# A fused vision and text kernel on Trainium2: the LoRA product of a tile as one float32r matmul over stacked high, low and high parts

## The chip, the cores and the metric

The kernel runs on one core of one Trainium2 chip. The metric is the device time of one execution in microseconds (us), median of the executions shown. Engines are called by the profile's names: PE is TensorE's matmuls and PEld its weight loads, DVE is VectorE, ACT is ScalarE, POOL is GpSimd, SP is SyncE, which issues all of the DMA transfers. Each engine works through its own list of instructions in order; semaphores tie the lists together.

## The reference

64 images are turned into nine window tokens and a class token each (a patch convolution and two small attentions), 77 text tokens are put behind them, and the 64 x 87 tokens of 256 channels run through one attention of 16 heads with residual and one feed-forward layer with residual. What the change touches is the LoRA part of that layer, with 8 experts of rank 4 and the best two of each token:

```python
logits = x @ gate_w.T
weights, idx = jax.lax.top_k(jax.nn.softmax(logits, axis=-1), 2)
base = x @ W_lin.T + b_lin
t = jnp.einsum('nd,nkdr->nkr', x, left[idx])
out_k = jnp.einsum('nkr,nkro->nko', t, right[idx])
lora = jnp.sum(weights[..., None] * out_k, axis=1)
return (base + lora).reshape(bsz, seq, -1)      # and h = h + this
```

## The kernel before

**Two halves.** The first, `patch_tokens`, makes the window and class tokens in 5 steps and writes them to DRAM. The second, `attention_ffn`, takes the tokens in 16 groups of 4 images: 348 tokens, as 3 tiles of 116. The two halves overlap from some 215 to 270 us; from there the program is the groups'.

**The order of the work** is written out by hand. For each engine there is a table of steps (`GROUP_PE`, `GROUP_DVE`, ...) with a name, a number k and a time; `play` sorts all steps of all groups by `GROUP_START` + 276 g + time, and that order is the engine's list. So an engine works on three or more groups in turn: beside the gate and the LoRA product of one group stand the scores of the next and the projections of the one behind. A step that waits holds up all that follows in its engine's list.

**The products.** Most matmuls are split: a high part (float32r) and a low part (the rest, float32r too) of both factors, and three products hi x hi, hi x lo, lo x hi, summed in PSUM (`mm_split`, L1358, with all its matmuls on L1355). Of a group, only the attention and the LoRA product (L1474) are plain fp32, where the profile counts two records for one matmul.

**A group's end**, step by step:

- `ffn` (PE L1355, ACT L1243): one product of 116x296 a tile gives the linear part, the 32 values x @ left of all experts and the 8 logits, into `f`.
- `logits`, `rank`, `weigh` (DVE L1312 to L1335): maximum, pairwise comparisons (`g_eq` L1318, `g_gt` L1319), ranks, weights `g_w` (L1330), and `tw` (L1332): the 32 values times the weight of their expert, 96 values for the three tiles side by side.
- `base` (POOL L1150) adds the linear part to the residual.
- `twT` (PE L1466, ACT L1255): one transpose of 116x96 for all three tiles, and its copy to SBUF. Its last row is ones and takes the bias.
- `lora.0`, `lora.1` (PE L1474): for each tile one product with K = 97. `right` has for each tile its own 97 x 256 block, in which only the 32 rows of that tile and the bias row are not zero. `lora.0` does tiles 0 and 1, `lora.1` tile 2, some 14 us later. All of it goes through one PSUM bank, C (`p_c`), which `proj`, `yT`, `ffn` and the gate share; `BANKS` and `take` make the waits.
- `out` (DVE L1344) adds the product to the residual, `store` (SP L1073) writes it.

Around it stand, on DVE, `rotate` (L1279, L1282, the rotary embedding of another group's tile), `max` (L1291), `norm` (L1298, L1299), `h2` (L1304) and `stats_c` (L1309, L1310); on PE, `mT` (L1405), `scores` (L1411, L1415), `pv` (L1427), `oN` (L1435), `qkT` (L1381) and `peak` (L1397), which waits for `place`, 8 transfers by SP; on ACT the copies `oT` (L1219) and `sq` (L1186); on POOL `add` (L1115).

## Time and profile before

| | us |
|---|---|
| median of the executions | 739.92 |
| all three | 743.48, 738.27, 739.92 |
| span of the profiled execution | 734.0 |
| what the median has beyond that span | 5.9 |
| chip, cores | one Trainium2, 1 core |

The profiled execution is listed by its span alone, from the first to the last instruction; its own device time lies around that and is not given apart, so the table sets the span against the median. The page gives for each engine its busy time as a share of the span, then the chain of work that ended last, followed back through what released each piece. The timeline gives start, duration, engine, line, tiles and shapes of single instructions or of short runs (x2, x4), and in brackets the engine's idle time before and what ended it. A matmul's duration overlaps with the next one's start, so what a matmul costs its engine is read from one start to the next.

### The profile page before, as it was taken

How to read it: one execution, taken by the hardware profiler on the slowest of the kernel's cores; microseconds unless marked ns; L12 is line 12 of the kernel's file. 1: busy time of each engine (PE TensorE's matmuls, PEld its weight loads, DVE VectorE, ACT ScalarE, POOL GpSimd, SP SyncE). 2: the span in 40 equal slices, each digit the busy share in tenths (PEclk: the TensorE clock that was granted, in tenths of full speed). 3: DMA queues.
4: the chain of work that ended last, by engine and by line, in shares of the span. 5: the costliest groups of instructions: out<-in, count | busy, mean ns of one | idle time of the engine just before them, and what ended most of it. 6: DMA issues, size and time to landing. Idle time of an engine off the chain costs nothing.

```text
span 734.0 us, 24407 instructions
## 1 busy us (share of the span) xinstructions
PE 673.9 (92%) x9431; PEld 564.8 (77%) x9431; DVE 531.2 (72%) x1192; ACT 432.0 (59%) x1115; POOL 491.0 (67%) x564
## 2 busy tenths in 40 slices
PE   5998998999985799999999999999999999999873
PEld 3987887888853577888888888888888888887652
DVE  2468687887978646788878878878878887866642
ACT  4553452635442346677777676677776777776541
POOL 3667563764648428787877877876976977975442
PEclk9999999999996969999999999999999999999996
DMA  8963472231011223223232332332332332122001
GB/s 222 237 163 116 129 224 47 54 83 44 22 24 40 59 54 79 63 70 82 67 78 73 75 83 73 79 82 72 78 83 68 79 86 67 42 54 62 26 25 34
DMA packets 69528, 58.73 MB, mean 80 GB/s; under 512 B 30607, under 2 KB 68646, under 8 KB 69286
## 3 DMA queue, kind: packets, MB, share of 16 engines
q1 hardware_dynamic: 69414, 57.18, 30.9%
q8 instruction: 76, 1.25, 0.7%
q14 instruction: 38, 0.31, 0.1%
HBM read 33.69 MB, written 11.40 MB: 61 GB/s over the span
## 4 chain that ended last, share of the span: by engine, by line
PE 71%; DVE 12%; issue 4%; ACT 4%; SPq 3%; POOL 3%; DMA 2%; POOLq 0%; DVEq 0%; ACTq 0%
PE p_a L1355 13%; PE p_c L1355 10%; PE p_conv L758 8%; PE p_kv L758 7%; PE p_o L1427 6%; PE p_s L1415 5%; PE p_mm L758 4%; PE p_s L1397 4%; PE p_n L1435 3%; PE p_c L1474 3%; PE p_a L1381 3%; PE p_s L1411 2%; DVE t L1282 2%; DMA kr<-qkT 2%; DVE kv L656 1%
## 5 line engine op out<-in xcount | busy, mean ns | idle before, releaser
L1291 DVE TENSOR_REDUCE mx<-p_s 87x16 bf16<-87x1392 f32 x64 | 102.5, 1602 | 44.6 <-PE p_s L1397 44.4
L1214 ACT ACTIVATE prT<-p_s 87x1392 f32<-87x1392 f32 x64 | 85.2, 1331 | 29.3 <-PE p_s L1415 27.8
L1121 POOL TENSOR_TENSOR t<-t,ss_rs 116x512 f32<-116x512 f32 x48 | 50.9, 1060 | 58.9 <-ACT ss_rs L1190 57.8
L426 POOL TENSOR_TENSOR xs_lo<-xcols,xs_hi 120x585 fp32r<-120x585 f32 (+1 forms) x45 | 60.4, 1348 | 43.7 <-ACT xs_hi L483 43.7
L1415 PE MATMUL p_s<-qr,kr 32*87 32x87 f32 x2048 | 68.8, 257 | 0.0
L1115 POOL TENSOR_TENSOR t<-t 116x512 f32<-116x512 f32 x48 | 62.4, 1299 | 5.6 <-DVE t L1282 5.6
L1135 POOL TENSOR_TENSOR yT_lo<-y_raw,yT_hi 128x232 fp32r<-128x232 f32 x48 | 32.5, 678 | 47.1 <-issue 31.4
L1124 POOL TENSOR_TENSOR t<-t,tabs 116x512 f32<-116x512 f32 x48 | 61.2, 1276 | 2.7
L1415 PEld LDWEIGHTS p_s<-qr,kr 32*87 32x87 f32 x2048 | 60.3, 154 | 0.0
L1411 PE MATMUL p_s<-mxT,pick_row 32*87 32x87 bf16 x1024 | 55.7, 208 | 1.9 <-ACT mxT L1208 1.9
L1427 PE MATMUL p_o<-prT,vp 87*32 87x87 f32 x2048 | 55.1, 248 | 0.1
L1427 PEld LDWEIGHTS p_o<-prT,vp 87*32 87x32 f32 x2048 | 43.9, 142 | 9.8 <-issue 3.2
L1130 POOL TENSOR_TENSOR onT_lo<-on_raw,onT_hi 128x174 fp32r<-128x174 f32 x64 | 37.0, 586 | 20.2 <-ACT onT_hi L1226 11.9
L1186 ACT ACTIVATE sq<-p_a 116x512 f32<-116x512 f32 x48 | 28.8, 600 | 36.5 <-PE p_a L1355 36.4
L440 POOL TENSOR_TENSOR red<-red,pe 117x256 f32<-117x256 f32 (+1 forms) x35 | 27.5, 785 | 31.9 <-ACT pe L491 30.9
L515 ACT COPY kv<-p_kv 117x512 f32<-117x512 f32 (+1 forms) x45 | 26.6, 590 | 30.9 <-PE p_kv L758 30.9
L1279 DVE TENSOR_TENSOR t<-p_a,tabs 116x512 f32<-116x512 f32 x48 | 32.9, 685 | 15.4 <-ACT sq L1186 15.4
L1435 PE MATMUL p_n<-ident,oT 128*87 128x128 f32 x256 | 40.2, 280 | 1.2 <-ACT onT_hi L1226 1.2
L1411 PEld LDWEIGHTS p_s<-mxT,pick_row 32*87 32x87 bf16 x1024 | 32.5, 117 | 11.5 <-issue 5.1
L1204 ACT ACTIVATE vt<-p_a,a_rs 116x256 f32<-116x256 f32 x48 | 22.6, 474 | 28.4 <-PE p_a L1355 28.4
L758 PE MATMUL p_conv<-w_conv_hi,xs_hi 120*117 120x256 f32 (+1 forms) x225 | 38.1, 299 | 0.0
L1397 PE MATMUL p_s<-kr,qr 32*87 32x88 f32 x1024 | 33.3, 256 | 4.3 <-ACT prT L1214 2.1
(287 smaller groups left out, 2077.8 us busy)
## 6 DMA issues: line engine op xcount, KB each, us to landing
xcols<-in_x_cols SPq DMA_DIRECT2D x12, 822.7 KB, 8.1
h<-h_tokens SPq DMA_DIRECT2D x16, 348.0 KB
out<-out_sb SPq DMA_DIRECT2D x48, 116.0 KB
h_tokens<-in_txt SPq DMA_DIRECT2D x4, 1232.0 KB, 8.7
x<-in_txt_cols SPq DMA_DIRECT2D x32, 154.0 KB, 4.1
qr<-qkT SPq DMA_DIRECT2D x64, 58.0 KB, 2.0
kr<-qkT SPq DMA_DIRECT2D x64, 58.0 KB, 2.0
vp<-vt SPq DMA_DIRECT2D x32, 87.0 KB
```

The source lines that it names most:

```text
L426: nc.gpsimd.tensor_tensor(xs.lo[:, n % XS_SLOTS, :, 0:M].bitcast(F32R), raw, xs.hi[:, n % XS_SLOTS, :, 0:M], ALU.subtract).then_inc(S['xs_ ...
L758: mm_ = nc.tensor.matmul(out, a, b, start=(c == 0), stop=(c == len(lhs) - 1))
L1115: link(nc.gpsimd.tensor_tensor(t1[:, b], t1[:, b], t2[:, b], ALU.add))
L1124: nc.gpsimd.tensor_tensor(by_head(t1[:, b]), by_head(t1[:, b]), table(2, k), ALU.add).then_inc(S['rope_ok'], 1)
L1214: nc.scalar.activation(prT[:, k % 2], p_s[0:SEQ, :, 0:QUADS * SEQ], ACT.Exp, scale=HD ** -0.5).then_inc(S['s_exp'], 1)
L1291: nc.vector.reduce_max(mx[:, k % 2, :, 0:QUADS], p_s[0:SEQ, :, 0:QUADS * SP].rearrange("p j (a k) -> p j a k", k=SP)[:, :, :, 0:SEQ], AX_X ...
L1355: mm_ = nc.tensor.matmul(out, a, b, start=(c == 0), stop=(c == len(lhs) - 1))
L1397: mm_ = nc.tensor.matmul(p_s[0:SEQ, j, a * SP:(a + 1) * SP], rows(qr, j, a, SEQ).bitcast(F32R), rows(kr, j, a, SP).bitcast(F32R), start=Tr ...
L1411: nc.tensor.matmul(p_s[0:SEQ, j, a * SEQ:(a + 1) * SEQ], pick_row[ROW * j:ROW * (j + 1), a], mxT[ROW * j:ROW * (j + 1), k % 2], start=True ...
L1415: mm_ = nc.tensor.matmul(p_s[0:SEQ, j, a * SEQ:(a + 1) * SEQ], rows(kr, j, a, SEQ), rows(qr, j, a, SEQ), start=False, stop=True, skip_grou ...
L1427: mm_ = nc.tensor.matmul(p_o[ROW * j:ROW * (j + 1), a * SEQ:(a + 1) * SEQ], vp[:, half, k, :, 4 * a + j], prT[:, k % 2, j, a * SEQ:(a + 1) ...
L1435: mm_ = nc.tensor.transpose(p_n[0:SEQ, c * P:(c + 1) * P], oT[:, k % 2, c], ident[:])
```

## The change

The LoRA product becomes float32r, high and low parts in one matmul. `tw` holds three copies of a tile's 32 values side by side (96 columns a tile), and each tile is transposed by itself, so that a tile's 96 rows stand ready in one column range of `twT`. ScalarE casts all 96 rows to float32r (the high part). VectorE's new step `tw_lo` writes the low part over rows 32 to 63. Two rows of ones take the bias. The other factor, `right_3`, holds high, high and low part of `right` and of the bias; it is made once. One float32r matmul with K = 98 is then high x high + low x high + high x low. `right` has one block in place of three.

```diff
--- before.py
+++ after.py
...
@@ -96,7 +97,7 @@
         self.w_v = Split(sb("w_v_hi", [P, CC, C]), sb("w_v", [P, CC, C]))
         self.w_p = sb("w_p", [P, CC, C])
         self.w_f = sb("w_f", [P, CC, FFN_N])
-        self.right = sb("right", [TILES * LR + 1, TILES, C])
+        self.right, self.right_hi, self.right_3 = (sb(n, [LORA_K, C]) for n in ("right", "right_hi", "right_3"))
         self.b_proj = sb("b_proj", [P, C])
         self.mean_row = sb("mean_row", [P, P])
         self.ones = sb("ones", [P, P])
...
@@ -129,17 +130,15 @@
         sp.dma_start(self.rope_in[:], io['rope']).then_inc(self.S['rope_in'], 16)
         sp.dma_start(self.rope_g[:], io['rope_g'].unsqueeze(0).broadcast_to([TP, 8, HD])).then_inc(self.S['rope_in'], 16)
 
-    LOADS = 3 + 1 + TILES + 1
+    LOADS = 3 + 1 + 3 + 1
 
     def load_weights(self, nc, sp, io):
         sources = (io['w_qkv'][:, 0:2 * C], io['w_qkv'][:, 2 * C:3 * C], io['w_ffn'], io['w_proj'])
         for w, source in zip(self.uncentred + [self.w_p[:]], sources):
             sp.dma_start(w, source.rearrange("(k p) n -> p k n", p=P)).then_inc(self.w_in, 16)
-        sp.wait_ge(self.S['zeroed'], 1)
-        for t in range(TILES):
-            sp.dma_start(self.right[LR * t:LR * (t + 1), t], io['right']).then_inc(self.w_in, 16)
-        sp.dma_start(self.right[TILES * LR:TILES * LR + 1], io['rows'][TOKEN_ROWS + 1:TOKEN_ROWS + 2].unsqueeze(1).broadcast_to(
-            [1, TILES, C])).then_inc(self.w_in, 16)
+        for n in range(3):
+            sp.dma_start(self.right[LR * n:LR * (n + 1)], io['right']).then_inc(self.w_in, 16)
+        sp.dma_start(self.right[3 * LR:LORA_K], io['rows'][TOKEN_ROWS + 1].unsqueeze(0).broadcast_to([2, C])).then_inc(self.w_in, 16)
 
     def fill_early(self, nc, pool, link):
 
@@ -149,7 +148,6 @@
         link(nc.gpsimd.memset(self.ident[:], 0.0))
         nc.gpsimd.affine_select(out=self.ident[:], in_=self.ident[:], compare_op=ALU.not_equal, fill=1.0, base=0,
                                 pattern=[[-1, P]], channel_multiplier=1).then_inc(self.S['filled'], 1)
-        nc.gpsimd.memset(self.right[:], 0.0).then_inc(self.S['zeroed'], 1)
 
     def fill_late(self, nc, pool, link):
 
@@ -913,7 +911,7 @@
 GROUP_DVE = table("""stats.0.-202 stats.1.-176 stats.2.-169 eps.0.-130 rotate.0.-17 ss.0.43 rotate.1.58 ss.1.114 rotate.2.173
                 ss.2.201 max.0.292 max.1.361 max.2.427 max.3.499 norm.0.522 norm.1.561 norm.2.603 norm.3.688
                 h2.0.733 h2.1.749 stats_c.0.791 stats_c.1.805 h2.2.861 stats_c.2.866 logits.0.950 rank.0.996
-                weigh.0.1038 out.0.1104 out.1.1109 out.2.1248""")
+                weigh.0.1038 tw_lo.0.1092 out.0.1104 out.1.1109 out.2.1248""")
 GROUP_PE = table("""qk.0.-48 qk.1.19 v.0.84 qkT.0.131 qk.2.148 qkT.1.194 v.1.211 qkT.2.277 peak.0.281 mT.0.315 scores.0.325
                 peak.1.353 mT.1.378 scores.1.388 pv.0.412 peak.2.419 mT.2.444 scores.2.453 oN.0.475 peak.3.482
                 pv.1.497 mT.3.520 pv.2.522 scores.3.529 oN.1.548 oB.0.569 oN.2.587 oB.1.611 pv.3.622 oB.2.651
...
@@ -981,8 +979,9 @@
         g_max, g_sum, g_rs = sb("g_max", [TP, TILES]), sb("g_sum", [TP, TILES]), sb("g_rs", [TP, TILES])
         g_e, g_rank, g_w = (sb(n, [TP, TILES, EXPERTS]) for n in ("g_e", "g_rank", "g_w"))
         g_gt, g_eq = (sb(n, [TP, TILES, EXPERTS, EXPERTS]) for n in ("g_gt", "g_eq"))
-        tw = sb("tw", [TP, TILES, LR])
+        tw = sb("tw", [TP, TILES, 3 * LR])
         out_sb = sb("out_sb", [TP, TILES, C])
+        twT = sb("twT", [LORA_K, TILES, TP])
 
         p_a = ps("p_a", [P, 512])
         p_s = ps("p_s", [P, 4, 512])
...
@@ -1089,7 +1088,6 @@
                 pool.wait_ge(W['stat'], CONVS)
                 pool.wait_ge(W['red'], (CELLS - 1) * STEPS)
                 ready(nc.gpsimd.memset(vp[:, :, :, HD:], 1.0))
-                ready(nc.gpsimd.memset(twT[TILES * LR:TILES * LR + 1], 1.0))
 
             def step(name, g, k):
                 half, b = g % 2, (3 * g + k) % 2
@@ -1143,6 +1141,15 @@
                         for n, (w, raw) in enumerate(((wp, w_p), (wf, w_f))):
                             pool.wait_ge(S['w2_high'], n + 1)
                             nc.gpsimd.tensor_tensor(w.lo[:].bitcast(F32R), raw[:], w.hi[:], ALU.subtract).then_inc(S['w2_low'], 1)
+                        pool.wait_ge(S['w2_low'], 2)
+                        pool.wait_ge(W['cls_ok'], STEPS)
+                        ready(nc.gpsimd.memset(twT[3 * LR:LORA_K], 1.0))
+                        pool.wait_ge(S['w2_high'], 3)
+                        lows = slice(2 * LR, LORA_K)
+                        ready(nc.gpsimd.tensor_tensor(right_3[lows].bitcast(F32R), right[lows], right_hi[lows], ALU.subtract))
+                        bias = slice(3 * LR, 3 * LR + 1)
+                        nc.gpsimd.tensor_copy(right_3[bias].bitcast(F32R), right_hi[bias]).then_inc(S['w2_low'], 1)
+                        pool.wait_ge(S['w2_low'], 3)
                     wait(pool, S['h2_ok'], 3 * (g - 1) + k + 1)
                     nc.gpsimd.tensor_tensor(hb[:, k], h[:, g % H_SLOTS, k], consts.b_proj[0:TP], ALU.add).then_inc(S['hb_ok'], 1)
                 if name == 'base':
@@ -1168,6 +1175,8 @@
                         act.wait_ge(consts.S['w_sub'], 3 * CC)
                         nc.scalar.copy(wp.hi[:].bitcast(F32R), w_p[:]).then_inc(S['w2_high'], 1)
                         nc.scalar.copy(wf.hi[:].bitcast(F32R), w_f[:]).then_inc(S['w2_high'], 1)
+                        nc.scalar.copy(right_3[0:2 * LR].bitcast(F32R), right[0:2 * LR])
+                        nc.scalar.copy(right_hi[:].bitcast(F32R), right[:]).then_inc(S['w2_high'], 1)
                     wait(act, S['a_var'], 3 * g + 3)
                     wait(act, S['v_out'], TILES * (g - 1))
                     link(nc.scalar.activation(a_ln[:, half], a_mv[:, half, :, 1], ACT.Ln, bias=eps5[0:TP, 0:1]))
@@ -1252,7 +1261,8 @@
                 if name == 'twT':
                     wait(act, S['twT_ok'], g + 1)
                     wait(act, S['lora'], 2 * g)
-                    nc.scalar.copy(twT[0:TILES * LR], product('gate', g, k)[0:TILES * LR, 0:TP]).then_inc(S['twT_out'], 1)
+                    nc.scalar.copy(twT[0:3 * LR].bitcast(F32R), product('gate', g, k)[0:3 * LR, 0:GT].rearrange("p (t n) -> p t n", t=TILES)
+                                   ).then_inc(S['twT_out'], 1)
 
             return step
 
@@ -1329,10 +1339,18 @@
                     link(nc.vector.reciprocal(g_rs[:], g_sum[:]))
                     link(nc.vector.tensor_tensor(g_w[:], g_w[:], g_rs[:].unsqueeze(2).broadcast_to([TP, TILES, EXPERTS]),
                                                  ALU.mult))
-                    nc.vector.tensor_tensor(
-                        tw[:].rearrange("p t (e r) -> p t e r", r=RANK),
-                        f[:, half, :, C:C + LR].rearrange("p t (e r) -> p t e r", r=RANK),
-                        g_w[:].unsqueeze(3).broadcast_to([TP, TILES, EXPERTS, RANK]), ALU.mult).then_inc(S['tw_ok'], 1)
+                    shape = [TP, 3, EXPERTS, RANK]
+                    for tile in range(TILES):
+                        last = nc.vector.tensor_tensor(
+                            tw[:, tile].rearrange("p (n e r) -> p n e r", n=3, r=RANK),
+                            f[:, half, tile, C:C + LR].rearrange("p (e r) -> p e r", r=RANK).unsqueeze(1).broadcast_to(shape),
+                            g_w[:, tile].unsqueeze(1).unsqueeze(3).broadcast_to(shape), ALU.mult)
+                    last.then_inc(S['tw_ok'], 1)
+                if name == 'tw_lo':
+                    dve.wait_ge(S['twT_out'], g + 1)
+                    lows = slice(LR, 2 * LR)
+                    nc.vector.tensor_tensor(twT[lows].bitcast(F32R), product('gate', g, k)[lows, 0:GT].rearrange("p (t n) -> p t n", t=TILES),
+                                            twT[lows], ALU.subtract).then_inc(S['tw_low'], 1)
                 if name == 'out':
                     dve.wait_ge(S['lora'], 2 * g + k // 2 + 1)
                     dve.wait_ge(S['fb_ok'], n3)
@@ -1461,17 +1479,20 @@
                     mm_split(product('tile', g, k)[0:TP, 0:FFN_N], yT.chunks(lambda x_, c: x_[:, b, c]), wf.chunks(lambda x_, c: x_[:, c])
                              ).then_inc(S['ffn'], 1)
                 if name == 'twT':
-                    use(bank('gate', g, k), S['twT_out'], g + 1)
+                    use(bank('gate', g, k), S['tw_low'], g + 1)
                     pe.wait_ge(S['tw_ok'], g + 1)
-                    nc.tensor.transpose(product('gate', g, k)[0:TILES * LR, 0:TP], tw[:].rearrange("p t n -> p (t n)"),
-                                        ident[0:TP, 0:TP]).then_inc(S['twT_ok'], 1)
+                    for tile in range(TILES):
+                        mm_ = nc.tensor.transpose(product('gate', g, k)[0:3 * LR, TP * tile:TP * (tile + 1)],
+                                                  tw[:, tile], ident[0:TP, 0:TP])
+                    mm_.then_inc(S['twT_ok'], 1)
                 if name == 'lora':
                     use(bank('lora', g, k), S['out_ok'], 3 * g + LORA_TILES[k][-1] + 1)
                     if g == 0 and k == 0:
-                        pe.wait_ge(S['set_0'], TW_SET)
-                    pe.wait_ge(S['twT_out'], g + 1)
+                        pe.wait_ge(S['w2_low'], 3)
+                    pe.wait_ge(S['tw_low'], g + 1)
                     for n, tile in enumerate(LORA_TILES[k]):
-                        mm_ = nc.tensor.matmul(product('lora', g, k)[0:TP, n * C:(n + 1) * C], twT[:], right[:, tile], start=True, stop=True)
+                        mm_ = nc.tensor.matmul(product('lora', g, k)[0:TP, n * C:(n + 1) * C], twT[:, tile].bitcast(F32R),
+                                               right_3[:].bitcast(F32R), start=True, stop=True)
                     mm_.then_inc(S['lora'], 1)
 
             return step
```

The order of the instructions around group 7's end, first TensorE at the transpose `twT` (the rows after the transpose are `mT`, `pv` and the first of `scores`), before:

```order
L1466 MATMUL p_c<-ident,tw 96x116 [waits b_tw_ok,b_yT_out]
L1405 MATMUL p_s<-ident_b,mx 128x87 [waits b_s_max]
L1427 MATMUL p_o<-prT,vp 32x87 [waits l_v_in0,l_v_in1,b_s_exp,b_o_out]
L1427 MATMUL p_o<-prT,vp 32x87 x15
L1411 MATMUL p_s<-mxT,pick_row 87x87 [waits b_mT_out]
```

and with the change:

```order
L1485 MATMUL p_c<-ident,tw 96x116 [waits b_tw_ok,b_yT_out]
L1485 MATMUL p_c<-ident,tw 96x116 x2
L1423 MATMUL p_s<-ident_b,mx 128x87 [waits b_s_max]
L1445 MATMUL p_o<-prT,vp 32x87 [waits l_v_in0,l_v_in1,b_s_exp,b_o_out]
L1445 MATMUL p_o<-prT,vp 32x87 x15
L1429 MATMUL p_s<-mxT,pick_row 87x87 [waits b_mT_out]
```

Two transposes more, and nothing else moved. Next TensorE at `lora.0` (ahead of it the end of `scores`, behind it `oN` and `qkT`), before:

```order
L1411 MATMUL p_s<-mxT,pick_row 87x87 x4
L1415 MATMUL p_s<-qr,kr 87x87 x4
L1474 MATMUL p_c<-right,twT 116x256 [waits b_twT_out]
L1474 MATMUL p_c<-right,twT 116x256
L1435 MATMUL p_n<-ident,oT 87x128 [waits b_o_out,b_o_norm]
L1435 MATMUL p_n<-ident,oT 87x128 x3
L1381 MATMUL p_a<-ident,t 128x116 [waits b_rope_ok,b_rot_ok]
```

and with the change:

```order
L1429 MATMUL p_s<-mxT,pick_row 87x87 x4
L1433 MATMUL p_s<-qr,kr 87x87 x4
L1494 MATMUL p_c<-right,twT 116x256 [waits b_tw_low]
L1494 MATMUL p_c<-right,twT 116x256
L1453 MATMUL p_n<-ident,oT 87x128 [waits b_o_out,b_o_norm]
L1453 MATMUL p_n<-ident,oT 87x128 x3
L1399 MATMUL p_a<-ident,t 128x116 [waits b_rope_ok,b_rot_ok]
```

The pair of products stands where it stood, and waits for `tw_low`, VectorE's new step, in place of ScalarE's copy. Last VectorE between `norm` and `out.0` (`c_st` is `stats_c`, `t` is `rotate`), before:

```order
L1298 RECIPROCAL rd<-p_n 87x16 [waits b_oB,b_oN]
L1299 TENSOR_TENSOR on<-p_n,rd 87x256 [waits k_dve_1]
L1309 BN_STATS c_st<-h 116x6 [waits b_h2_ok]
L1310 BN_AGGR c_mv<-c_st 116x2 [waits k_dve_1]
L1279 TENSOR_TENSOR t<-p_a,tabs 116x512 [waits b_qkT_ok,b_sq_ok]
L1282 TENSOR_TENSOR t<-p_a,tabs 116x32x8 x2
L1344 TENSOR_TENSOR out_sb<-p_c,h 116x256 [waits stored0,b_fb_ok,b_lora]
```

and with the change:

```order
L1308 RECIPROCAL rd<-p_n 87x16 [waits b_oB,b_oN]
L1309 TENSOR_TENSOR on<-p_n,rd 87x256 [waits k_dve_1]
L1319 BN_STATS c_st<-h 116x6 [waits b_h2_ok]
L1320 BN_AGGR c_mv<-c_st 116x2 [waits k_dve_1]
L1289 TENSOR_TENSOR t<-p_a,tabs 116x512 [waits b_qkT_ok,b_sq_ok]
L1292 TENSOR_TENSOR t<-p_a,tabs 116x32x8 x2
L1352 TENSOR_TENSOR twT<-p_c,twT 32x348 [waits b_twT_out]
L1362 TENSOR_TENSOR out_sb<-p_c,h 116x256 [waits stored0,b_fb_ok,b_lora]
```

`tw_lo` (L1352) has come in behind `rotate` and ahead of `out.0`.

## Rows read from the trace of the kernel before

**Rows 1.** The page, parts 1 and 4: busy us (share of the span) xinstructions; chain shares.

```profile
PE 673.9 (92%) x9431; PEld 564.8 (77%) x9431; DVE 531.2 (72%) x1192; ACT 432.0 (59%) x1115; POOL 491.0 (67%) x564
...
PE 71%; DVE 12%; issue 4%; ACT 4%; SPq 3%; POOL 3%; DMA 2%; POOLq 0%; DVEq 0%; ACTq 0%
```

**Rows 2.** One stretch: length, busy PE, PEld, DVE, ACT, POOL, clock, DMA share, GB/s.

```profile
330.00:640.00 310.00, 306.83 (x5564) 261.87 (x5560) 252.35 (x571) 224.26 (x581) 244.89 (x297) 1.00 0.29 75
```

**Rows 3.** Waits, 330 to 640 us: total us, times, longest.

```profile
DVE h L1304 <- PE p_c L1355: 11.6, 11, 1.1
DVE out_sb L1344 <- PE p_c L1474: 8.1, 11, 0.8
...
PEld p_s L1397 <- issue: 1.6, 4, 0.6
...
PE p_s L1397 <- DMA kr<-qkT: 0.7, 2, 0.4
```

**Rows 4.** Timeline, TensorE's matmuls: start us, us, engine, line, xcount [idle before <-releaser].

```profile
520.49 0.49 PE L1355 MATMUL p_c<-w_p_hi,onT_hi 128*116 128x256 f32 x2 [0.19 <-DVE h L1304]
520.82 0.40 PE L1355 MATMUL p_c<-w_p_lo,onT_hi 128*116 128x256 f32 x2
521.05 0.41 PE L1355 MATMUL p_c<-w_p_hi,onT_lo 128*116 128x256 f32 x2
...
526.24 0.26 PE L1466 MATMUL p_c<-ident,tw 116*96 116x116 f32 x1
526.34 0.20 PE L1405 MATMUL p_s<-ident_b,mx 87*128 87x87 bf16 x1
...
528.30 1.12 PE L1474 MATMUL p_c<-right,twT 97*116 97x256 f32 x4
529.26 0.60 PE L1435 MATMUL p_n<-ident,oT 128*87 128x128 f32 x4
...
542.64 0.60 PE L1474 MATMUL p_c<-right,twT 97*116 97x256 f32 x2
543.08 0.56 PE L1381 MATMUL p_a<-ident,t 116*128 116x116 f32 x4
```

**Rows 5.** Timeline, VectorE, 519 to 531 us and at 670 us.

```profile
523.92 0.26 DVE L1332 TENSOR_TENSOR tw<-f,g_w 116x96 f32<-116x96 f32 x1
524.09 1.60 DVE L1291 TENSOR_REDUCE mx<-p_s 87x16 bf16<-87x1392 f32 x1
...
527.34 0.69 DVE L1279 TENSOR_TENSOR t<-p_a,tabs 116x512 f32<-116x512 f32 x1
527.95 0.75 DVE L1282 TENSOR_TENSOR t<-p_a,tabs 116x256 f32<-116x256 f32 x2
529.46 0.76 DVE L1344 TENSOR_TENSOR out_sb<-p_c,h 116x256 f32<-116x256 f32 x2 [0.76 <-PE p_c L1474]
...
669.88 0.76 DVE L1344 TENSOR_TENSOR out_sb<-p_c,h 116x256 f32<-116x256 f32 x2 [1.62 <-PE p_c L1474]
```

**Rows 6.** Lines L1330, L1319 (ns min/median/max); timeline of GpSimd.

```profile
L1330 DVE TENSOR_TENSOR g_w<-g_w,g_rs x16: 182/946/990, 325.4 to 723.8; 116x24 f32<-116x24 f32 x16
...
L1319 DVE TENSOR_TENSOR g_gt<-f x16: 350/651/655, 316.3 to 721.1; 116x192 f32<-116x192 f32 x16
...
521.33 0.72 POOL L1150 TENSOR_TENSOR h<-h,f 116x256 f32<-116x256 f32 x1
...
522.52 1.32 POOL L1115 TENSOR_TENSOR t<-t 116x512 f32<-116x512 f32 x1
523.92 0.86 POOL L1150 TENSOR_TENSOR h<-h,f 116x256 f32<-116x256 f32 x1
```

**Rows 7.** Timeline, ScalarE, the copies twT and oT.

```profile
527.20 0.26 ACT L1255 COPY twT<-p_c 96x116 f32<-96x116 f32 x1
527.39 0.45 ACT L1219 COPY oT<-p_o 128x348 f32<-128x348 f32 x1
```

**Rows 8.** Timeline, TensorE in group 14.

```profile
711.74 1.09 PE L1474 MATMUL p_c<-right,twT 97*116 97x256 f32 x4 [0.43 <-ACT twT L1255]
```

11 lines of the change are left out of this document (6 added, 5 removed).

## The prediction

> **What bounds the kernel now.** I read the page first. TensorE is busy 92% of the span and carries 71% of the chain that ended last [rows 1]. Nearly all of the change's work lies in the group stage, so the stretch of 330 to 640 us comes next: there TensorE is busy 306.8 of 310.0 us at full clock, VectorE 252.4, ScalarE 224.3, GpSimd 244.9 [rows 2]. TensorE has no idle time to speak of; the others have some. The waits of that stretch (11 group periods of some 28 us) say where [rows 3]: VectorE waits for TensorE at the projection's `h2` (1.06 us a group) and at the LoRA product (0.74 us a group), and TensorE waits for the `place` transfers before `peak` in a few groups, 0.7 us seen on the matmuls and 1.6 us on the weight loads.
>
> So a shorter LoRA product is worth its time only if its inputs are there. That is asked of the timeline of one group. TensorE starts `twT` at 526.24, reaches `lora.0` at 528.30 and leaves it at 529.26 [rows 4]. VectorE, which has no part between `tw` and the LoRA product before the change, is at that moment in `rotate`: its three instructions run from 527.34 to 528.70, and the first of them follows on other work without a gap [rows 5]. The place repeats from group to group: VectorE's wait for the product is 0.74 us in the mean of 11 groups and at most 0.8 [rows 3]. The new step `tw_lo` stands in VectorE's list between that `rotate` and `out.0`, and `lora.0` waits for it.
>
> **TensorE.** Before, a product of 116x256 is two records; a pair of products holds the engine from 528.30 to 529.26, 0.96 us, and the single one of `lora.1` from 542.64 to 543.08, 0.44 us [rows 4]. A float32r product of the same 256 columns is there in the projection: two take 0.23 us from 520.82 to 521.05, and 0.33 us where they come out of a wait (520.49 to 520.82) [rows 4]. So `lora.1` gives back 0.44 - 0.12 = 0.32 us, `lora.0` 0.96 - 0.23 = 0.73 us if it finds its input ready, 0.63 us if it waits. Two more transposes a group cost 0.10 us each (526.24 to 526.34) [rows 4]. Without any wait that is 0.32 + 0.73 - 0.20 = 0.85 us a group and 13.6 us in 16.
>
> **ScalarE.** The copy `twT` grows from 116 to 348 columns: 0.26 to 0.45 us, the latter being the time of the `oT` copy of 348 columns [rows 7]. It ends near 527.9 instead of 527.46. VectorE is in `rotate` until later, so this costs nothing in a steady group. In group 14, whose steps follow one another, it costs its 0.19.
>
> **VectorE: `tw`.** One instruction of 96 elements becomes three. They follow one another at 0.17 us (523.92 to 524.09) [rows 5]: +0.34 us. The bare price is not all. `g_w` of 24 elements takes 0.18 us at its least and 0.95 at the median of 16, and in the steady group `tw`, which waits for it, starts at 523.92, just behind the end of GpSimd's `add` at 522.52 + 1.32 = 523.84 [rows 5, 6]. `g_gt` takes 0.35 us at its least and 0.65 at the median, again in groups with GpSimd at work, and it is the second of two instructions issued together [rows 6]. Right at `tw` GpSimd starts `base` (523.92) and needs 0.86 us where the instruction before it of the same line took 0.72 [rows 6]: it was held 0.14 us by `tw`. I read it so: an instruction of VectorE that reads two operands from SBUF, and one of GpSimd, keep each other out, and one that has been waiting goes ahead of VectorE's next. Then the first `tw` goes, `base` follows it, and the second `tw` waits for most of 0.72 us. Bounds are 0 and 0.77 (what `g_w` loses); from the nearest case, `g_gt`, which loses 0.30 us to a GpSimd instruction of two thirds of the size, I take 0.50. Together `tw` makes VectorE 0.84 us later in each of the groups 0 to 11.
>
> This is also what the Trainium skill says, page SBUF — State Buffer, section Who interferes with whom: an instruction of VectorE with two inputs in SBUF contends with one of GpSimd that reads SBUF, and the second to issue is blocked until the first has finished; `tw_lo` and `out` read one operand from PSUM and are free of it. The rows on `g_w` and `g_gt` agree. Without this rule the sum would be the second case below, with it the first.
>
> **VectorE: `tw_lo`.** It reads 348 elements from PSUM. By `out_sb` (two of 256 in 0.76, so 0.42 for one) and `rotate`'s first (512 in 0.69) [rows 5] it takes 0.42 + 92 x 0.27/256 = 0.52 us.
>
> **The wait.** In the row's group, before: `rotate` starts 527.34 and its successor could start 1.29 us later. Now: 527.34 - 0.03 (it waited for nothing longer) + 0.84 = 528.15, `tw_lo` from 529.44 to 529.96, TensorE 0.06 us behind, as after a late `h2`, so `lora.0` at 530.02 and the next step at 530.35 instead of 529.26: **+1.09 us**. TensorE alone would have been at `lora.0` at 528.50; the other 1.5 us it stands still. Queued behind are `oN`, `qkT`, `peak` and the projection. `peak` has waits of its own for the transfers of `place`, whose start doesn't move; of these waits, 0.7 to 2.3 us in all, I let 1.6 be swallowed. VectorE is later by about 1.1 us at `max.0` too, but it waits 1 us or more for TensorE twice before the group ends [rows 3], so nothing is carried over. A steady group is thus longer by 1.09 - 0.32 = 0.77 us: 12 x 0.77 - 1.6 = **+7.6 us**.
>
> **The tail.** Groups 12 and 13 have no `rotate` ahead; VectorE waits 1.62 us for the product there [rows 5]. Between 0 and -0.85 us each; I take -0.35, as half lies beside a wait for a transfer. In group 14 TensorE waits for the copy `twT` [rows 8], so its chain runs through every added piece: +0.34 and 0.50 (`tw`), 0.20, 0.19, 0.58 (`tw_lo` and its signal), less 0.63: **+1.2 us**. In group 15 the same additions, near 1.8, meet the three products at the end of the program, which give back some 1.1 and more at a lower clock: 0, within 0.9. Sum of the tail: +0.5.
>
> **Setup.** ScalarE makes two more copies and GpSimd three small instructions, once, and GpSimd is busy 67% of the span [rows 1]; the memset of `right` goes and as many transfers stay. At most 3 x 0.72 = 2.2 us by `base`'s row [rows 6], at least 0; I take 0, for GpSimd's own waits cover it, and keep the rest for the range.
>
> **Sum: +8.1 us.** The profiled execution spans 734.0 us, 5.9 less than the median of the runs; I carry the difference over: 739.9 + 8.1 = **748.0 us**. Case ends: with 0 for the held `tw` the steady group is 0.50 us less, with 0.77 it is 0.27 more: 742.0 and 751.2; rounding the transfers' share and the setup in, 741 to 753.
>
> **Rivals.**
> 1. **The three `tw` are not held** by `base`. Then a steady group changes by +0.27 us, group 14 by +0.7: 12 x 0.27 - 1.6 + 0 = +1.6, **741.6 us**. For it: `tw` itself shows 0.26 us and went ahead of `base`. Against: `g_gt`, in the same position, is held in most groups. Chance 0.27.
> 2. **The saving arrives**, the other side. The place is `rotate`'s end: if VectorE finished `tw_lo` by 528.44, 1.5 us before my figure, TensorE would not wait, and all of 0.85 us a group would come: 726.3 us. Half of that way is plausible: a GpSimd a little later would neither hold `g_w` (0.77 us) nor `tw` (0.50), leaving `lora.0` at 528.75 and a group shorter by 0.18 + 0.32 = 0.50 us: -6.0 with -0.7 for groups 12 and 13, **733.2 us**. It decides where VectorE is ahead by over 0.77 us of my figure. For it: TensorE is the busiest engine and loses 17 us of work. Against: offsets that repeat in 12 groups, with `g_w` held every time. Chance 0.15.
> 3. **A second hold**: GpSimd's next instruction, moved by the first, meets the third `tw` or the pushed `max` and `norm`, 0.5 us more a group: **754 us**. Against: GpSimd is idle a fifth of the stretch [rows 2], so another instruction need not stand ready. Chance 0.13.
>
> My forecast has 0.45. That the products aren't cheaper isn't a case: the same form runs in the projection [rows 4].
>
> **Numbers.** Under 1% (7.4 us) a measurement of this kernel can't be told from no change. The forecast lies at its edge: of its 0.45, 0.26 is slower and 0.19 the same. Rival 1: the same, 0.01 to slower, 0.02 to faster. Rival 2: 0.10 faster, 0.05 the same. Rival 3: slower, 0.13. Faster 0.12, same 0.48, slower 0.40. The forecast's own range is 741 to 753; to hold 8 in 10, with half of the second rival and of the third, it is 733 to 755.
>
> **What would show it.** Right: in most groups TensorE idles over 1 us before the LoRA pair, released by `tw_lo`; records of that line fall to a half; the second `tw` takes near 0.7 us and the others 0.26; `base` still 0.86; VectorE's wait before `out_sb` all but gone; the group period up from 310.0/11 = 28.2 us by 0.8. Wrong: a wait under 0.5 us before the pair (rival 2), `tw` at 0.26 three times and the wait near 1.0 (rival 1), or TensorE waiting for `max` as well (rival 3). What would upset it most is `tw_lo` being done before `rotate`'s end, or a chain of waits that runs through another step of the group than this one.

## The result, and the profile after

The changed kernel takes **771.96 us** (median of 4 runs, 769.02 to 773.53) against 740.54 us (738.27 to 743.48); the ratio is 1.045, 95% interval 1.0403 to 1.0497. Ratios are of fast executions alone, so they differ a little from those of the medians (here 1.042). The kernel is slower, as the likeliest case had it, but by 31.4 us and not by 8.1, and outside the range. The profiled execution spans 769.8 us, 35.8 more than before.

The page, parts 1, 2 and 4 (the clock is in tenths of full speed, one digit for a fortieth of the span), to be read against [rows 1]:

```profile
span 769.8 us, 24428 instructions
PE 684.3 (89%) x9415; PEld 575.4 (75%) x9415; DVE 557.0 (72%) x1240; ACT 433.8 (56%) x1117; POOL 492.3 (64%) x565
...
PEclk9999999999988689999899899999899999999875
...
PE 62%; DVE 23%; issue 6%; ACT 4%; POOL 2%; DMA 2%; SPq 1%; DVEq 0%; POOLq 0%; ACTq 0%
```

VectorE's share of the chain that ended last has risen from 12% to 23%. And the clock row shows an 8 at several places in the group stage, where before it was 9 throughout. The stretches (length, busy PE, PEld, DVE, ACT, POOL, clock, DMA share, GB/s), the first against [rows 2], then three groups from one transpose `twT` to the next, and the second of them in part:

```profile
330.00:640.00 310.00, 290.17 (x5118) 247.42 (x5117) 249.88 (x555) 205.75 (x533) 225.42 (x272) 0.95 0.28 71
330.30:359.80 29.50, 27.52 (x510) 23.47 (x509) 24.74 (x56) 20.53 (x53) 22.39 (x28) 1.00 0.29 74
359.80:392.50 32.70, 30.41 (x509) 25.99 (x508) 25.03 (x56) 20.51 (x53) 22.32 (x28) 0.90 0.25 65
392.50:421.90 29.40, 27.50 (x509) 23.48 (x508) 24.63 (x56) 20.52 (x53) 22.38 (x28) 1.00 0.30 76
...
364.00:371.00 7.00, 6.53 (x39) 5.72 (x40) 4.90 (x10) 1.50 (x6) 2.30 (x4) 0.51 0.28 77
```

So there are two kinds of group. Five of eleven take 29.4 to 29.5 us at a clock of 1.00, which is 1.2 more than 28.2; six take 30.9 to 32.7 us at 0.89 to 0.94. In the longest, TensorE stands still from about 362.6 to 364.5 us (1.83 us, 0.35 more than in the others), and from the end of that standstill it works for some 7 us at half clock (1.2 instead of 2.4 GHz). At full clock the work of those 7 us would have taken about half of the time. The group is 3.3 us longer than its neighbours: 0.35 for the longer standstill and some 2.9 for the clock.

The waits of the stretch (total us, times, longest), against [rows 3]:

```profile
PE p_c L1494 <- DVE twT L1352: 15.1, 10, 1.8
DVE h L1314 <- PE p_c L1373: 10.6, 10, 1.1
DVE out_sb L1362 <- PE p_c L1494: 7.2, 10, 0.9
PEld p_s L1423 <- DVE mx L1301: 6.3, 17, 0.6
PE p_s L1423 <- DVE mx L1301: 2.8, 11, 0.3
```

The first row is the predicted wait: 1.5 us a group, in every group, released by `tw_lo`. The last two rows are `mT` waiting for `max`; before, there were 0.5 us of that in the stretch, on the weight loads alone. VectorE in one steady group, from the projection's `h2` to `out`, against [rows 5]:

```profile
387.79 0.42 DVE L1314 TENSOR_TENSOR h<-p_c,hb 116x256 f32<-116x256 f32 x1 [1.06 <-PE p_c L1373]
...
388.81 0.41 DVE L1338 SCALAR_TENSOR_TENSOR g_w<-g_rank,g_e 116x24 f32<-116x24 f32 x1
389.25 0.18 DVE L1339 RECIPROCAL g_rs<-g_sum 116x3 f32<-116x3 f32 x1
389.46 1.00 DVE L1340 TENSOR_TENSOR g_w<-g_w,g_rs 116x24 f32<-116x24 f32 x1
390.50 1.14 DVE L1344 TENSOR_TENSOR tw<-f,g_w 116x96 f32<-116x96 f32 x3
391.56 1.59 DVE L1301 TENSOR_REDUCE mx<-p_s 87x16 bf16<-87x1392 f32 x1
...
394.78 0.67 DVE L1289 TENSOR_TENSOR t<-p_a,tabs 116x512 f32<-116x512 f32 x1
395.37 0.75 DVE L1292 TENSOR_TENSOR t<-p_a,tabs 116x256 f32<-116x256 f32 x2
396.15 0.51 DVE L1352 TENSOR_TENSOR twT<-p_c,twT 32x348 fp32r<-32x348 f32 x1
397.31 0.76 DVE L1362 TENSOR_TENSOR out_sb<-p_c,h 116x256 f32<-116x256 f32 x2 [0.65 <-PE p_c L1494]
```

From `h2` to the start of the `rotate` it is 6.99 us, before 5.84 (521.50 to 527.34). The three `tw` take 1.14 us together (predicted 1.10), `tw_lo` 0.51 (0.52). What I had not priced is the first `g_w`, 0.41 instead of 0.18 us. TensorE's end of it, against [rows 4]:

```profile
392.52 0.46 PE L1485 MATMUL p_c<-ident,tw 116*96 116x116 f32 x3
393.22 0.21 PE L1423 MATMUL p_s<-ident_b,mx 87*128 87x87 bf16 x1 [0.23 <-DVE mx L1301]
...
396.81 0.47 PE L1494 MATMUL p_c<-right,twT 98*116 98x256 f32 x2 [1.49 <-DVE twT L1352]
397.11 0.60 PE L1453 MATMUL p_n<-ident,oT 128*87 128x128 f32 x4
```

The pair of products holds TensorE for 0.30 us instead of 0.96, but it stands behind a standstill of 1.49 us.

Where the 35.8 us lie, by the starts of `twT`: 2.0 had been lost when the first group reached it (330.30 against 328.34), 26.4 in the next eleven groups, 7.4 in the rest. The 26.4 divide into 12.9 (eleven groups of 29.45 us in the mean of the undisturbed five, less 311.06 us) and 13.5 (what the six groups at low clock are longer than 29.45).

### The profile page after: what moved, and what is told of

The parts are those of the page before. It is cut to its first block, busy times and chain, and to the rows that moved or that the text cites. A ratio compares the mean times of both kernels' runs of the same rounds, so it can differ in the third digit from the quotient of the medians.

```text
span 769.8 us, 24428 instructions
## 1 busy us (share of the span) xinstructions
PE 684.3 (89%) x9415; PEld 575.4 (75%) x9415; DVE 557.0 (72%) x1240; ACT 433.8 (56%) x1117; POOL 492.3 (64%) x565
## 3 DMA queue, kind: packets, MB, share of 16 engines
q1 hardware_dynamic: 69412, 57.18, 29.4%
## 4 chain that ended last, share of the span: by engine, by line
PE 62%; DVE 23%; issue 6%; ACT 4%; POOL 2%; DMA 2%; SPq 1%; DVEq 0%; POOLq 0%; ACTq 0%
PE p_a L1373 12%; PE p_c L1373 10%; PE p_conv L756 7%; PE p_kv L756 5%; PE p_s L1433 4%; PE p_mm L756 4%; PE p_o L1445 4%; PE p_s L1415 3%; PE p_n L1453 3%; DVE mx L1301 3%; DVE t L1292 3%; PE p_a L1399 2%; DVE tw L1344 2%; DVE g_w L1340 2%; PE p_s L1429 1%
## 5 line engine op out<-in xcount | busy, mean ns | idle before, releaser
L1433 PE MATMUL p_s<-qr,kr 32*87 32x87 f32 x2048 | 70.5, 261 | 0.0
L1133 POOL TENSOR_TENSOR yT_lo<-y_raw,yT_hi 128x232 fp32r<-128x232 f32 x48 | 32.7, 683 | 52.7 <-issue 31.1
L438 POOL TENSOR_TENSOR red<-red,pe 117x256 f32<-117x256 f32 (+1 forms) x35 | 27.5, 785 | 31.5 <-ACT pe L489 30.5
L1289 DVE TENSOR_TENSOR t<-p_a,tabs 116x512 f32<-116x512 f32 x48 | 32.7, 682 | 15.9 <-ACT sq L1195 15.7
L1453 PE MATMUL p_n<-ident,oT 128*87 128x128 f32 x256 | 42.9, 293 | 1.2 <-ACT onT_hi L1235 1.2
L1204 ACT COPY qkT<-p_a 128x464 f32<-128x464 f32 x48 | 26.1, 543 | 29.4 <-PE p_a L1399 29.3
L1373 PE MATMUL p_a<-w_qk_hi,xT_hi 128*116 128x512 f32 x96 | 38.0, 480 | 1.0 <-ACT qkT L1204 0.6
```

What stands on the lines that cost most here:

```text
L1373: mm_ = nc.tensor.matmul(out, a, b, start=(c == 0), stop=(c == len(lhs) - 1))
L1433: mm_ = nc.tensor.matmul(p_s[0:SEQ, j, a * SEQ:(a + 1) * SEQ], rows(kr, j, a, SEQ), rows(qr, j, a, SEQ), start=False, stop=True, skip_grou ...
L1453: mm_ = nc.tensor.transpose(p_n[0:SEQ, c * P:(c + 1) * P], oT[:, k % 2, c], ident[:])
```

## The experiments

Twelve kernels. **Theory W**: the late `tw_lo` makes TensorE stand still, which costs its length, and a standstill of that length also lets the clock fall, which costs about as much again. **Rival L**: the clock falls because there is less TensorE work, or for a cause outside the wait. Ratios are to the kernel before, on the same chip, with a 95% interval.

**1. `tw_lo` ahead of the `rotate`.**

```diff
-                weigh.0.1038 tw_lo.0.1092 out.0.1104
+                weigh.0.1038 tw_lo.0.1086 out.0.1104
```

> The changed kernel with one number altered: tw_lo stands in VectorE's list ahead of the rotate instead of behind it. In the changed kernel's trace a group takes 29.4 us where the granted clock is 1.00 throughout and 30.9 to 32.7 us in six of eleven groups, in which the clock falls to 0.50 right in or behind the 1.5 us that TensorE stands still before the LoRA pair. Theory W (the standstill costs its own length, and it also brings the clock down): tw_lo ends 0.5 us after the copy twT, TensorE waits under 0.2 us, no group runs at the low level, a group takes 27.6 to 28.0 us and the kernel 730 to 738 us. Rival L (the clock falls because TensorE has less work a group, or for a cause outside this wait): the wait goes, 1.2 us a group come back, but some groups still run at 0.50 and the kernel takes 750 to 758 us. Rival Q (the rotate, now 0.5 us later, delays qkT or max by as much as is won): a group stays at 28.6 us or more at full clock, 744 us or more.

749.44 us, ratio 1.0074 (1.0025 to 1.0124). One number takes the loss from 4.5% to 0.7%. Clock and waits of the stretch:

```profile
330.00:640.00 310.00, 298.07 (x5465) 252.42 (x5463) 265.76 (x595) 220.16 (x570) 239.55 (x292) 1.00 0.29 74
```
```profile
PE p_a L1399 <- DVE t L1292: 4.3, 11, 0.4
PE p_s L1423 <- DVE mx L1301: 2.8, 11, 0.3
PE p_c L1494 <- DVE twT L1352: 2.2, 10, 0.2
```

No group of the stretch is at the low level, as W says and L denies. But a group takes 28.75 us, not 27.8: rival Q. TensorE now waits 0.4 us for the `rotate`, 0.25 for `max`, 0.2 for `tw_lo`, together nearly a microsecond a group, so at this place too VectorE's added work is paid for.

**2. A first try to fill the standstill.**

```diff
+                    if k == 0:
+                        for n in range(12):
+                            nc.tensor.matmul(product('lora', g, k)[0:TP, 0:C], wp.hi[:, 0, 0:TP]..., wp.hi[:, 0]..., ...)
                     pe.wait_ge(S['tw_low'], g + 1)
```

> The changed kernel with twelve float32r products of 116x256 on constant weights ahead of lora.0, into the columns that lora.0 then overwrites; TensorE works through the 1.4 us in which it stood still, all waits and data stay. Theory W: the lateness of tw_lo is unchanged, so a group stays at 29.4 us, but the clock stays at 1.00 in 330 to 640 us; the 13.8 us of the long groups and some 4 us of the tail go, 752 to 758 us. Rival L (another cause of the low clock): groups of 31 to 33 us remain, 768 us or more. If the fillers themselves delay lora.0 (over 1.5 us long), each 0.1 us costs 1.5 us in all.

776.71 us, ratio 1.0475 (1.0398 to 1.0551). A miss of construction: `use` ahead of the fillers already waits for `tw_low`, as the bank is the gate's. The wait of 1.38 us stayed and the fillers came behind it, so a group at full clock is 30.7 us and the three at a low clock are 32.1 to 32.7. As a test of W the run says nothing. But that the clock was 1.00 in eight of eleven groups here, with the standstill in all of them, is the first sign that the standstill alone doesn't decide.

**3. One `tw` in place of three.**

```diff
-                    for tile in range(TILES):
-                        last = nc.vector.tensor_tensor(tw[:, tile]..., f[:, half, tile, C:C + LR]..., g_w[:, tile]..., ALU.mult)
+                    link(nc.vector.tensor_tensor(g_wr[:]..., g_w[:].unsqueeze(3)..., g_rs[:]..., ALU.mult))
+                    nc.vector.tensor_tensor(tw[:]..., f[:, half, :, C:C + LR].unsqueeze(2)..., g_wr[:].unsqueeze(2)..., ALU.mult)
```

> The changed kernel with the weights spread to 96 elements in the last g_w instruction, so that one tw instruction of 288 elements takes the place of three of 96. Theory H (the second tw is held by GpSimd's base for about 0.5 us): g_w and tw together take 0.6 us less, the wait before lora.0 falls from 1.5 to 0.9 us, a full-clock group from 29.4 to 28.8 us. With the clock still falling in half the groups that is 760 to 765 us; if a standstill of 0.9 us no longer brings it down, 745 to 750 us. Rival (three instructions were slow by themselves, not held): the one instruction gives 0.2 us a group or less, 768 us or more.

766.36 us, ratio 1.0343 (1.0268 to 1.0418). The 0.6 us did not come. In a steady group:

```profile
383.98 1.08 DVE L1342 TENSOR_TENSOR g_wr<-g_w,g_rs 116x96 f32<-116x96 f32 x1
385.10 0.98 DVE L1345 TENSOR_TENSOR tw<-f,g_wr 116x288 f32<-116x288 f32 x1
```

The one `tw` is issued just behind GpSimd's `base` (385.02) and held as a whole; in the tail, where no `base` runs, the same instruction takes 0.46 us. So the hold is real, but folding three into one doesn't evade it. TensorE still stands 1.47 us, and nine of eleven groups ran at 0.89 to 0.94, where the changed kernel with the same standstill had six.

**4. The wait alone, in the kernel before.**

```diff
+                if name == 'late':
+                    dve.wait_ge(S['twT_out'], g + 1)
+                    nc.vector.tensor_tensor(spare[:], product('gate', g, k)[0:LR, 0:TP]..., twT[0:LR]..., ALU.subtract)...
-                    pe.wait_ge(S['twT_out'], g + 1)
+                    pe.wait_ge(consts.S['zeroed'], g + 2)
```

> The kernel before, with its fp32 products, its one tw and its one transpose, and one thing added: an instruction of VectorE of tw_lo's size (32x348, one operand from PSUM, result unused) at tw_lo's place behind the rotate, and both LoRA products wait for it. No work of TensorE changes. Its end should come at 0.98 us behind the point at which TensorE reaches lora.0. Theory W: TensorE stands still 0.9 to 1.0 us a group, a full-clock group takes 29.0 to 29.2 us, and the clock falls in some groups as in the changed kernel: 757 to 770 us. Rival L (the low clock comes from the smaller products): the wait costs its length only, 750 to 753 us, clock 1.00 in the group stage.

752.95 us, ratio 1.0147 (1.0073 to 1.0222). TensorE waits 0.87 us in a group, a group is 29.06 us, and the clock is 1.00 in all eleven. By this run alone L was alive: a wait without lighter products, and no low clock.

**5. The work of `tw` alone, in the kernel before.**

```diff
+                    for n in range(2):
+                        nc.vector.tensor_tensor(spare[:, n]..., f[:, half, :, C:C + LR]..., g_w[:]..., ALU.mult)
```

> The kernel before with two more instructions of tw's size and inputs ahead of tw (results unused), so that VectorE has the three that the change gives it; TensorE's work, the transposes and the LoRA products stay fp32 and wait for what they waited for. It tests the step of my forecast by which lateness of VectorE is not carried over while it doesn't meet the LoRA wait. If that holds: the second instruction is held by base as in the changed kernel (three in 1.1 us), mT waits 0.1 to 0.2 us for max in a group, a group takes 28.2 to 28.4 us, 740 to 745 us. Rival (VectorE and TensorE form a loop from h2 to the rotate and mT in which any VectorE work costs its length): a group of 28.8 us or more, 750 us or more.

747.03 us, ratio 1.0116 (1.0049 to 1.0183). The least of its groups are 28.49 us, 0.3 more than 28.15, with TensorE never waiting for anything in the LoRA step. "Nothing is carried over" is off by at least 0.3 us a group, between the two expectations and nearer to the first. The mean of the eleven is 28.81 us against 28.28 before, but this trace is of the longest execution (754.35 us) and has two waits for transfers, 0.63 and 1.16 us, in it.

**6. The wait doubled.**

```diff
-                    nc.vector.tensor_tensor(spare[:]..., ALU.subtract).then_inc(consts.S['zeroed'], 1)
+                    for n in range(2):
+                        last = nc.vector.tensor_tensor(spare[:, n]..., ALU.subtract)
+                    last.then_inc(consts.S['zeroed'], 1)
```

> The fourth kernel (before, plus an unused instruction of tw_lo's size that the LoRA products wait for) with two such instructions instead of one. That one stood TensorE still for 1.0 us a group, its groups took 29.06 us at a granted clock of 1.00. Now the standstill is 1.5 us, as long as in the changed kernel, while all of TensorE's products are those of before. Theory W (the length of the standstill decides whether the clock falls): some groups of 31 to 33 us beside groups of 29.5 us, mean clock in 330 to 640 us 0.95, 766 us or more. Rival L (the clock falls only with the lighter float32r products): all groups 29.5 us at 1.00, 757 to 762 us.

767.15 us, ratio 1.0327 (1.0239 to 1.0415). The trace is of the longest of the four executions, 771.14 us; the shortest took 757.65. Three groups:

```profile
448.60:478.10 29.50, 28.00 (x511) 23.91 (x510) 23.83 (x55) 20.44 (x53) 22.37 (x28) 1.00 0.29 75
507.60:540.90 33.30, 31.29 (x510) 26.39 (x509) 24.69 (x58) 20.61 (x53) 22.31 (x28) 0.90 0.25 65
570.40:602.50 32.10, 29.85 (x510) 25.09 (x509) 24.62 (x58) 20.51 (x53) 22.30 (x28) 0.95 0.25 68
```

All of TensorE's work is the fp32 work of before, and the clock falls in three of eleven groups: L is refuted as far as lighter products go. The standstill is 1.3 us in most groups and 1.6 to 1.8 in four; the three low groups are among the four. The group behind the eleven is low too (0.94), with a standstill of only 1.31 us. In the first of the three, VectorE, TensorE, and the clock us by us:

```profile
503.86 1.33 DVE L1329 SCALAR_TENSOR_TENSOR g_w<-g_rank,g_e 116x24 f32<-116x24 f32 x1
```
```profile
511.77 1.09 PE L1482 MATMUL p_c<-right,twT 97*116 97x256 f32 x4 [1.76 <-DVE spare L1341]
```
```profile
511.00:512.00 1.00, 0.23 (x1) 0.26 (x2) 0.63 (x2) 0.41 (x1) 1.00 (x3) 1.00 0.21 60
512.00:513.00 1.00, 1.00 (x7) 0.83 (x7) 0.10 (x1) 0.00 (x0) 1.00 (x1) 1.00 0.11 35
513.00:514.00 1.00, 1.00 (x11) 0.71 (x13) 0.97 (x4) 0.06 (x1) 0.18 (x1) 0.68 0.12 38
514.00:515.00 1.00, 1.00 (x18) 0.92 (x19) 0.56 (x2) 0.89 (x3) 0.00 (x0) 0.50 0.23 65
```

A `g_w` of 24 elements took 1.33 us, beside a GpSimd `add` that began with it, where it takes 0.17 in the groups around; the standstill grew to 1.76, and only after it the clock fell. The order in time excludes that the low clock makes the wait.

**7. The standstill filled.**

```diff
+                if name == 'lora' and k == 0 and g < GROUPS - 3:
+                    for bank_ in BANKS['N']:
+                        pe.wait_ge(*freed[bank_])
+                    for n in range(11):
+                        nc.tensor.matmul(p_n[0:TP, 0:C], wp.hi[:, 0, 0:TP]..., wp.hi[:, 0]..., start=True, stop=True)
```

> The changed kernel with eleven float32r products of 116x256 on constant weights, some 1.3 us, ahead of lora.0 in TensorE's list, this time into the bank of the transposed outputs, which is free then, so that they don't wait for tw_lo (in the first try they stood behind that wait). tw_lo comes when it came. Theory W: the wait left before lora.0 is 0.2 to 0.4 us, the groups take 29.4 us throughout at a clock of 1.00, 752 to 758 us. Rival (the clock falls for another reason than the standstill): groups of 31 us and more stay, 768 us or more.

756.32 us, ratio 1.021 (1.0133 to 1.0287). The stretch, and one group:

```profile
330.00:640.00 310.00, 305.51 (x5466) 262.32 (x5463) 259.13 (x581) 215.52 (x558) 233.66 (x285) 1.00 0.29 73
416.30:445.70 29.40, 28.98 (x520) 24.86 (x519) 24.62 (x56) 20.49 (x53) 22.40 (x28) 1.00 0.29 74
```

This is the separating run. Nothing is faster: `tw_lo` is as late, a group takes 29.3 to 29.8 us. Only TensorE is busy where it stood still, with work that nobody uses, and all eleven groups keep 1.00. By the ratios the loss falls from 4.5% to 2.1%; the medians, 771.96 and 756.32, lie 15.6 us apart. Of the 18.8 us by which this trace is longer than the one before the change, 12.6 are the lateness itself, in the eleven groups, and 6.9 lie behind them, where the last three groups have no fillers and the clock falls again (the first `twT` comes 0.6 us earlier).

**8. A candidate.** As 1 and 3 together, and `weigh` behind `max.3`, so that `g_w` and `tw` don't meet GpSimd's `add` and `base`.

```diff
-                weigh.0.1038 tw_lo.0.1092 out.0.1104
+                weigh.0.1052 tw_lo.0.1086 out.0.1104
```

> A candidate: tw_lo ahead of the rotate, one tw of 288 elements with the weights spread to 96, and weigh behind max.3 instead of ahead of it, so that VectorE makes max (which reads PSUM) while GpSimd's add runs, and g_w is not held 0.8 us by it. In e1 a group takes 28.75 us with mT waiting 0.25 us for max and qkT 0.4 us for the rotate. If g_w and tw are no longer held, VectorE is 1 us a group shorter, these waits go, and a group takes 27.6 to 28.0 us: 728 to 738 us, faster than before. If they are held all the same (by base, which follows add), or twT now waits for tw, 28.3 to 28.8 us: 742 to 750 us.

743.82 us, ratio 1.0005 (0.9957 to 1.0053): as before, and not the 728 to 738 us that were hoped for. In a group:

```profile
555.25 0.36 DVE L1339 SCALAR_TENSOR_TENSOR g_w<-g_rank,g_e 116x24 f32<-116x24 f32 x1
...
555.86 0.26 DVE L1342 TENSOR_TENSOR g_wr<-g_w,g_rs 116x96 f32<-116x96 f32 x1
556.15 0.46 DVE L1345 TENSOR_TENSOR tw<-f,g_wr 116x288 f32<-116x288 f32 x1
```

1.08 and 0.98 us have become 0.26 and 0.46. A group takes 28.0 us, 0.2 less than before, but three of the last ones lose 7.4 us (27.7, 28.0 and 23.4 against 26.8, 26.1 and 18.8), with waits for `tw` of 1.1 and 1.5 us and clocks of 0.94 and 0.64 in the last two of them.

**9. The same with `weigh` at its old place in the last four groups.**

```diff
-    turns += [(GROUP_START + GROUP_PERIOD * g + time, ...)
+    turns += [(GROUP_START + GROUP_PERIOD * g + (1038 if name == 'weigh' and g >= GROUPS - 4 else time), ...)
```

> e8_reordered with weigh at its old place in the last four groups. e8's steady groups take 28.01 us against 28.2 of the kernel before, but its last groups are longer (27.7, 28.0 and 23.4 us against 26.8, 26.1 and 18.8), where TensorE waits for tw 1.1 and 1.5 us, since max now stands ahead of it and no add of GpSimd is there any more to be avoided, and where the clock is 0.94 and 0.64. Expected: the waits for tw go in these groups, 2 to 7 us less than e8: 736 to 741 us, a ratio to before of 0.990 to 0.998. If the lower clock of the end doesn't come from these waits (TensorE also waits 1.2 and 1.4 us for max there, in every kernel of the study), less than 2 us are won: 741 to 744 us.

742.24 us, ratio 1.0018 (0.9977 to 1.0058), 1.6 us below experiment 8 by the medians, which is the expectation's second case and within the noise. The waits for `tw` are gone (26.7 us for the first of these groups), but two later ones stay long (28.7 and 20.1) at clocks of 0.88 and 0.85. One steady group of this kernel, beside its neighbour, and TensorE's waits in that neighbour:

```profile
411.90:439.90 28.00, 27.43 (x509) 23.40 (x509) 23.24 (x54) 20.52 (x53) 22.24 (x28) 1.00 0.30 78
439.90:470.90 31.00, 29.13 (x510) 24.84 (x510) 23.50 (x54) 20.51 (x53) 22.25 (x28) 0.94 0.29 73
```
```profile
PE p_s L1415 <- DMA kr<-qkT: 1.3, 1, 1.3
PE p_a L1399 <- DVE t L1294: 0.4, 1, 0.4
```

A wait of 1.3 us for a `place` transfer, in a kernel whose LoRA product doesn't wait, and the clock falls within a microsecond behind it. The cause need not be `tw_lo`; a standstill of that size can do it.

**10. `qkT.2` behind `peak.0`.**

```diff
-                qk.2.148 qkT.1.194 v.1.211 qkT.2.277 peak.0.281
+                qk.2.148 qkT.1.194 v.1.211 qkT.2.282 peak.0.281
```

> e9 with qkT.2 behind peak.0 in TensorE's list. In e8 TensorE waits 0.39 us a group there for the rotate that tw_lo now stands ahead of. If that wait is on the path, a group falls from 28.0 to 27.6 or 27.7 us, 4 us less than e9: 731 to 737 us. If max.0, or the place transfers that follow qkT, then come too late, 28.0 us or more, and no gain.

749.28 us, ratio 1.0123 (1.0075 to 1.0171). The wait for the `rotate` is gone, and a group still takes 28.04 us: TensorE waits instead for the exponential (3.7 us in the stretch) and for the transfers, which start later (5.4 us in five places, the longest 1.5, with the clock at 0.94 in that group).

**11. The changed kernel with `weigh` behind `max.3` and nothing else.**

```diff
-                weigh.0.1038 tw_lo.0.1092 out.0.1104
+                weigh.0.1052 tw_lo.0.1092 out.0.1104
```

> The changed kernel with one number altered: weigh stands behind max.3 in VectorE's list; three tw instructions and tw_lo behind the rotate stay. Theory H (of the lateness of tw_lo, 0.24 us at the first g_w, 0.8 at the last, and 0.5 at tw are VectorE held by GpSimd's add and base): out of add's way these go, tw_lo ends 1.3 to 1.5 us earlier, TensorE waits at most 0.3 us for it, the clock stays at 1.00 and a group takes 27.9 to 28.2 us: 740 to 747 us with the longer tail of e8. Rival (base holds them at the new place as well): wait 0.7 to 1.0 us, 28.8 us, 748 to 755 us.

752.54 us, ratio 1.0151 (1.0084 to 1.0219); the trace is of the longest execution, 758.87 us. The time lies where the rival had it, but not for the rival's reason. The holds at the last `g_w` and at `tw` are gone:

```profile
535.04 0.42 DVE L1338 SCALAR_TENSOR_TENSOR g_w<-g_rank,g_e 116x24 f32<-116x24 f32 x1
...
535.70 0.18 DVE L1340 TENSOR_TENSOR g_w<-g_w,g_rs 116x24 f32<-116x24 f32 x1
535.92 0.60 DVE L1344 TENSOR_TENSOR tw<-f,g_w 116x96 f32<-116x96 f32 x3
```

1.00 us is 0.18 and 1.14 us is 0.60, so 1.36 us of VectorE were GpSimd's doing, 0.54 of it new with the change. Yet TensorE still waits 1.15 us. VectorE now waits 0.47 us for `max`'s own input, so that from `h2` to the `rotate` it is 6.21 us, only 0.78 less than in the changed kernel, and that is also what a group is shorter (28.6 us for 29.4). Of the eleven, the one with a wait of 1.5 us ran at low clock.

**12. The order of 9 in the kernel before**, a control.

> The kernel before with weigh behind max.3 except in the last four groups, as in e9: a control that says how much of e9's time is due to the order and not to the LoRA change. TensorE is busy 28.0 of 28.2 us there, so freeing VectorE can give at most 0.2 us a group: 738 to 742 us, ratio 0.995 to 1.002.

741.77 us, ratio 1.0031 (1.0002 to 1.006). The order gives nothing where TensorE is the bound. So 9 and 12 are level: with the float32r products in the best order I found, the LoRA change is worth nothing measurable. This run also shows the low clock without any part of the change. In one group TensorE waits for a `place` transfer, and the group takes 31.5 us where its neighbours take 28.2 and 28.5:

```profile
415.93:447.46 31.53, 29.61 (x510) 25.04 (x509) 22.52 (x52) 20.56 (x53) 22.17 (x28) 0.95 0.28 71
```
```profile
PE p_s L1398 <- DMA kr<-qkT: 1.7, 1, 1.7
```

What the kernels show together, for the eleven groups from the first `twT` on:

| kernel | usual longest standstill of a group, us | groups under 1.00 |
|---|---|---|
| before | 0.2, once 0.4 | 0 |
| 7, filled | 0.2, twice 0.3 | 0 |
| 5, `tw` alone | 0.2, once 1.16 | 0 |
| 12, order alone | 0.2, once 1.72 | 1 (that one) |
| 1, `tw_lo` first | 0.4, once 0.5 | 0 |
| 8, candidate | 0.4, once 0.7 | 0 |
| 9, tail order | 0.4, once 1.31 | 1 (that one) |
| 10, `qkT` later | 0.6, once each 1.01 and 1.23, once 1.52 | 1 (the last) |
| 4, wait alone | 0.87, once 1.24 | 0 |
| 11, `weigh` behind | 1.15, once 1.50 | 1 (that one) |
| 6, wait doubled | 1.30, four of 1.60 to 1.77 | 3 (of the four) |
| 2, fillers behind | 1.38, once 1.73 | 3 (that one and two more) |
| 3, one `tw` | 1.47 | 9 |
| changed kernel | 1.48, once 1.83 | 6 (that one and five more) |

No group whose longest standstill is under 1.3 us is at a low clock. In all 25 low groups the clock falls in a standstill of 1.31 us or more, or within 2 us of its end.

## Why the prediction was wrong

**Right**: that the saving would not arrive, and why. In every steady group TensorE stands before the LoRA pair for `tw_lo`; the wait was put at 1.5 us and is 1.48. The pair holds TensorE for 0.30 us, for 0.96 before. The second `tw` was held by `base` (three in 1.14 us, 1.10 predicted), `base` still takes 0.86, and experiment 11 shows the hold by taking `add` and `base` away. `tw_lo` takes 0.51 us against 0.52. VectorE's wait before `out_sb` did not vanish as I wrote: 0.65 us instead of 0.76, since VectorE now waits there for the pair that its own `tw_lo` has only just released. (Where the prediction says which of its cases goes with a hold and which without, it counts loosely: with a hold it is the forecast, without it rival 1.)

**The step that failed** is the price of the wait. The sum took "the other 1.5 us it stands still" at its length and left the clock at the 1.00 of [rows 2]. In the trace the clock falls in six of eleven groups in that standstill or just behind it, which is 13.5 us, and more in the tail. Experiments 6 and 7 separate it: standstills of 1.6 us and more bring low groups with all the old work in place, and the changed kernel with the standstill filled has none in these eleven and is 15.6 us faster. No rival held this case. The profiled execution is 35.8 us longer where 8.1 were forecast; 13.5 of the 27.7 us between are here. The kernel before had the low level in its rows too, at 0.83 between 210 and 300 us and at 0.82 and 0.50 in its last two groups; the prediction thought of it at the program's end alone.

**A second term was too small**: a steady group was to be 0.77 us longer, less what transfers' waits swallow, and is 1.2. From `h2` to the `rotate` VectorE is 1.15 us later, not 0.84 less 0.03. The rows name 0.23 us at the first `g_w`, 0.05 at the second, 0.04 at `tw`; `tw_lo` starts 1.37 us behind the `rotate` and not 1.29, and TensorE 0.15 us behind its end and not 0.06. The 0.23 is "a second hold", my third rival, on an instruction I hadn't looked at, and that rival's sign, TensorE waiting for `max` as well, is there with 0.25 us a group. For the hold: GpSimd stands 0.3 us later against VectorE than before, and its `onT_lo` (388.61 to 389.18) meets `g_w`. That `onT_lo` is what holds it rests on the overlap alone; in experiment 11 the first `g_w` still took 0.42, with `base` (534.68 to 535.42) then beside it.

**"Nothing is carried over"** held only nearly. Experiment 5 puts `tw`'s work into the kernel before, where no LoRA step waits for it, and finds 0.3 us a group. The prediction leaned on two waits of 1 us or more by [rows 3]; these rows have 1.05 us at `h2` and 0.74 at the LoRA product. Both waits are still there after the change (1.06 and 0.65 us), but between them stands `mT`, which waits for `max`; that this is how the 0.3 us get through is argued from the rows and not tested.

**The 1.6 us swallowed** by the waits for transfers: TensorE's matmuls have no wait for a transfer left in 330 to 640 us, as foreseen (0.7 us before, on `peak`). It is inside the 12.9.

**The tail**, +0.5 predicted, +6.2 measured; the 7.4 above include group 11, which the prediction counts as steady (28.05 us for 26.8). Group 12 is 28.4 us instead of 26.1, at a clock of 0.88, and group 13 21.1 instead of 18.8, at 0.84. Group 14, forecast at +1.2, is 1.7 longer, and group 15, forecast at 0, is 0.2 shorter. In group 12 TensorE waits 1.2 and 1.4 us for `max`, in the kernel before too, where the clock stayed at 1.00; in nine of the twelve experiments it fell in that group, in 2, 7 and the control (12) it didn't. How much of the 6.2 us belongs to the change stays open.

**Setup**, 0 predicted, +2.0: the first matmul starts 0.27 us later (8.23 for 7.96). The rest is mostly the clock of this execution: the first `twT` comes anywhere between 323 and 335 us in the fourteen traces, and it goes with the mean clock from 210 to 300 us, a part ahead of the first LoRA product. That clock is 0.92 in the earliest trace (experiment 2), 0.83 before, 0.81 after the change, and 0.75 in the latest (experiment 10). So single profiled executions can differ by several us for a reason outside the change.

## What to carry to other kernels

Where TensorE is busy nearly all the time at full clock, price a new wait twice: its length, and the work that follows it at half clock. Look for the longest standstill that the profile before shows without a loss of clock (here 0.4 us in the eleven groups, 1.4 in the tail), and treat a longer one as unknown, not as free. A saving on the busiest engine whose inputs cost another engine some 1.7 us a group needs that time to be idle at that very place; the order tables decide that, and moving one step (experiment 1) was worth 22.5 us by the medians, against the 13.6 that the whole change could have given.

## What the hardware showed that I had not expected

- **The clock can fall after a standstill of 1.3 us in an engine that is otherwise busy**, but not in all groups alike: with 1.48 us in every group, six of eleven; with the same standstill in experiment 3, nine; with 0.87 us, none (table above). In experiment 2, with 1.38 us in every group and more work behind it, three, all in the first 97 us of the stage. I draw no threshold from this; other things than the length play a part, and which they are is open. In these groups a low stretch lasts some 3 or some 7 us and costs a little under half of itself (groups of 30.9 and of 32.2 to 32.7 us beside 29.45). The Trainium skill, page TensorE: Matmul & The Clock Gate, section HAM oscillation — how this bites in real kernels, describes such a pattern, a kernel that falls to the low level at each wait for a transfer and loses half of the time spent there. The 7.0 us at 0.51, with some 2.9 us lost, come near to that price. The waits of its example are 3 to 5 us, longer than any standstill in these groups.
- **The clock sets the spread between runs of one kernel.** Experiment 8's ten runs go from 735.5 us (mean clock 0.968) to 750.2 us (0.939), in the order of their clocks by and large. So a difference of 1% between two such kernels needs many runs.
- **An instruction of GpSimd that waits goes ahead of VectorE's next two-operand one, however short that is.** A `g_w` of 24 elements takes 1.00 us behind `add` (389.13 to 390.43) and 0.18 us out of its way; one `tw` of 288 elements takes 0.98 us behind `base` and 0.46 without. The hold is what is left of the other engine's instruction: folding three into one did not help (experiment 3), another order did (8 and 11). That GpSimd's turn comes between is seen at `tw`: `base` starts with the first of the three (390.50) and takes 0.86 us for its usual 0.74, and the second takes 0.80 us where the first takes 0.26 and the third 0.25.
